# An attention kernel on one core: the weighted sum and the work-bank task change places in three of four slots

## The reference

```
q = heads(x @ Wq);  k_s, v_s = heads(x @ Wkv_short);  k_l, v_l = heads(x @ Wkv_long)
decay_bias = -|i - j| * (1 - decay_factor)
out = alpha * softmax(q k_s^T / 4 + decay_bias) v_s + (1 - alpha) * softmax(q k_l^T / 4) v_l
x = layernorm(x + out @ Wo)
c = sigmoid(xt wf + c uf + bf) * c + sigmoid(xt wi + c ui + bi) * tanh(xt wc + c uc + bc)   # over the 16 sequences
x = layernorm(x + tanh(x wo + c_final uo + bo))
```

## Time and profile before

| | |
|---|---|
| median of 3 runs | 2131.12 us (2130.34 to 2136.34) |
| the profiled execution, its own time | 2128.4 us |
| its span | 2126.6 us |
| PE busy | 2004.9 us (94%) |
| DVE busy | 1532.1 us (72%) |
| ACT busy | 1458.0 us (69%) |
| POOL busy | 254.4 us (12%) |
| exponential, 128x1024, without and with bias unit scale | 1024 and 1114 ns |
| maximum, 128x1024 | 1221 ns |
| `keep_sums` copy, `vals` copy, `kq_h` copy | 598, 383, 593 ns |
| `kq_l` | 691 ns |

### The profile page before, as it was taken

One profiled execution on the slowest core, in us unless ns is written; L12 is line 12 of the kernel. 1 busy time (PEld: TensorE's weight loads), 2 busy tenths in 40 slices (PEclk: granted clock), 3 DMA queues, 4 the chain that ended last, 5 costly groups with the idle time before them and its releaser, 6 DMA issues.

```text
span 2126.6 us, 40587 instructions
## 1 busy us (share of the span) xinstructions
PE 2004.9 (94%) x15776; PEld 1055.1 (50%) x15776; DVE 1532.1 (72%) x1826; ACT 1458.0 (69%) x1750; POOL 254.4 (12%) x284
## 2 busy tenths in 40 slices
PE   6999999999999999999999999999999878999997
PEld 3444444444444444444444444444444336888887
DVE  6777878878787878787878787878787743333346
ACT  2777777777777777777777777777777662333337
POOL 0001111111111111111111111111111011000014
PEclk7999999999999999999999999999999999999999
DMA  4233333333333333333333333333323411000017
GB/s 112 63 78 77 87 77 87 78 87 78 86 79 85 80 85 79 85 80 85 81 84 80 84 82 83 82 85 81 84 70 86 114 53 40 30 30 31 30 61 257
DMA packets 157060, 170.00 MB, mean 80 GB/s; under 512 B 72756, under 2 KB 92980, under 8 KB 156868
## 3 DMA queue, kind: packets, MB, share of 16 engines
q1 hardware_dynamic: 132740, 133.61, 25.2%
q10 hardware_dynamic: 24128, 33.79, 5.1%
HBM read 54.55 MB, written 17.83 MB: 34 GB/s over the span
## 4 chain that ended last, share of the span: by engine, by line
PE 74%; ACT 8%; issue 6%; DVE 6%; SPq 4%; DMA 1%; ACTq 1%; POOL 0%; DVEq 0%; POOLq 0%
PE pv_ps L772 15%; PE work L676 14%; PE pair_ps L708 14%; PE banks L1163 12%; PE pair_ps L734 12%; ACT probs L443 7%; DVE maxes L633 3%; PE pair_ps L684 3%; PE banks L1203 2%; SPq L241 2%; DVE stats L619 1%; DVE res L615 1%; SPq L246 1%; SPq L303 1%; PE banks L1210 1%
## 5 line engine op out<-in xcount | busy, mean ns | idle before, releaser
L633 DVE TENSOR_REDUCE maxes<-pair_ps 128x2 fp32r<-128x1024 f32 x1024 | 1228.0, 1221 | 294.4 <-PE pair_ps L684 164.6
L443 ACT ACTIVATE probs<-pair_ps,small 128x1024 f32<-128x1024 f32 x512 | 563.4, 1114 | 221.3 <-PE pair_ps L684 218.7
L443 ACT ACTIVATE probs<-pair_ps 128x1024 f32<-128x1024 f32 x512 | 513.2, 1024 | 113.9 <-PE pair_ps L708 105.4
L772 PE MATMUL pv_ps<-probs,vals 128*32 128x512 f32 x4096 | 548.7, 608 | 11.1 <-ACT pv_sb L477 10.8
L708 PE MATMUL pair_ps<-q_op,k_op 56*128 56x512 f32 (+1 forms) x2048 | 479.8, 477 | 31.1 <-DVE maxes L633 16.2
L734 PE MATMUL pair_ps<-k_op,q_op 55*128 55x512 f32 x2048 | 451.7, 440 | 40.6 <-ACT probs L443 26.0
L708 PEld LDWEIGHTS pair_ps<-q_op,k_op 56*128 56x128 f32 (+1 forms) x2048 | 193.0, 185 | 461.8 <-DVE maxes L633 219.7
L734 PEld LDWEIGHTS pair_ps<-k_op,q_op 55*128 55x128 f32 x2048 | 196.8, 187 | 213.5 <-issue 105.1
L684 PE MATMUL pair_ps<-eye_b,tri_b 64*128 64x64 bf16 x4096 | 164.3, 194 | 0.0
L684 PEld LDWEIGHTS pair_ps<-eye_b,tri_b 64*128 64x128 bf16 x4096 | 94.9, 96 | 116.2 <-issue 97.7
L772 PEld LDWEIGHTS pv_ps<-probs,vals 128*32 128x32 f32 x4096 | 81.3, 108 | 112.5 <-issue 98.5
(11 more groups left out here) (148 smaller groups left out, 2080.4 us busy)
## 6 DMA issues: line engine op xcount, KB each, us to landing
k_op<-kq_h SPq DMA_DIRECT2D x508, 64.0 KB, 2.2
q_op<-kq_h SPq DMA_DIRECT2D x256, 64.0 KB, 2.3
o_att<-pv_sb SPq DMA_DIRECT2D x512, 32.0 KB
inverses<-inv_dram SPq DMA_DIRECT2D x64, 256.0 KB
k_op<-kq_l SPq DMA_DIRECT2D x254, 64.0 KB, 2.3
x_step<-in_xT ACTq DMA_DIRECT2D x16, 512.0 KB, 4.2
q_op<-kq_l SPq DMA_DIRECT2D x128, 64.0 KB, 2.3
q_op<-shift_rows SPq DMA_DIRECT2D x512, 2.0 KB
```

The lines of the kernel that those rows point to most:

```text
L443: act.activation(probs[:, s % 2, 2 * hp:2 * hp + 2, :], pairs_ps[pair_of(b, s, "b", hp)][:, :, :], ACT.Exp, scale=LAM if s // 4 % 2 else 1 ...
L633: dve.reduce_max(maxima[u % 2][:, :, hp, s % 4], pairs_ps[pair_of(b, s, "a", hp)][:, :, :], mybir.AxisListType.X).then_inc(a_reduced, 1)
L772: last = pe.matmul(pv_ps[32 * h:32 * h + 32, :], vals[:, c, g // 2, att, at:at + 32], probs[:, s % 2, h, :], start=(c == 0), stop=(c == TC ...
```

## The change

In the slots with c = 0, 2 and 3, PE issues `weigh_before` where `work_task` stood (behind the scores of pair 0) and `work_task` where `weigh_before` stood (behind the scores of pair 1). The part of the slot with c = 1 stays. On ACT the task's part goes behind the exponential of pair 1. On DVE it goes behind the maximum of pair 1 in every slot (it stood there already with c = 0).

```diff
@@ ACT, body
                     if exists(b):
                         exp_pair(b, s, 0)
-                    part_or_values(b, s)
                     if exists(b):
                         exp_pair(b, s, 1)
+                    part_or_values(b, s)
@@ DVE, body
                     reduce(0)
                     if s % TC == 0:
                         turn(*unit_of(b, s // 4 + 1))
-                        reduce(1)
+                    reduce(1)
                     if has_task(b, s):
...
-                    if s % TC:
-                        reduce(1)
@@ PE, body
                     bias_for_max(b, s, 0)
-                    work_task(b, s)
+                    weigh_before(b, s)
                     scores(b, s, 1)
                     scores_for_max(b, s, 1)
                     bias(b, s, 1)
                     bias_for_max(b, s, 1)
-                    weigh_before(b, s)
+                    work_task(b, s)
...
                     bias_for_max(b, s + 2, 0)
-                    work_task(b, s + 2)
+                    weigh_before(b, s + 2)
                     scores(b, s + 2, 1)
...
-                    weigh_before(b, s + 2)
+                    work_task(b, s + 2)
                     scores(b, s + 3, 0)
...
-                    work_task(b, s + 3)
+                    weigh_before(b, s + 3)
                     scores(b, s + 3, 1)
...
-                    weigh_before(b, s + 3)
+                    work_task(b, s + 3)
```

## The result

The changed kernel takes 2152.8 us (median of 4 runs, 2152.11 to 2153.02), against 2130.7 us for the one before (2128.41 to 2136.34): by the means 1.0099 times as long, 95% interval 1.0079 to 1.0119. The forecast was 2152.6 us, +21.5 where +22.1 came. The profiled execution took 2153.0 us, its span 2151.2.

What follows compares the result with a forecast made beforehand. The prediction took PE as the bound. Its terms sum to 1.4 us per sequence, 21 us over fifteen, plus 0.5 in the last: 2131.1 + 21.5 = 2152.6 us; own range 2145 to 2167.

Steps and rivals of the forecast that it cites:

- PE is the bound, and small standstills add up: PE, whole sequence: it stands still about 6 us per sequence in small pieces, and small delays are not made good later.
- The new V adds no wait for its exponential: PE, V issued 1.6 us earlier: the fill ahead already needed the same exponential, so added wait 0.
- the fills lose and gain 0.1 us by V and W and come out at 0: PE fills: those with W in place of V lose 0.1 us, others gain it; in odd units 0 net.
- The copy ahead of `keep_sums` in slots 24 and 28: ACT: the moved copy delays keep_sums and chunk 1's exponentials, +0.35 us in slot 24 and +0.3 in slot 28.
- the relief of b2.1: PE, units 8, 24 and 28: b2.1's lateness behind a late exponential goes with V1 ahead of it, -0.1 us each.
- The same in slots 0 and 4: ACT: the moved copy delays keep_sums, +0.3 us in slot 0 and +0.2 in slot 4.
- My step for slot 4: ACT: keep_sums goes from 805.65 to 806.05, but the next exponential had 0.18 us of waiting: +0.2 us.
- The `kq_h` copy ahead of b0.0's exponential: ACT, between b3.1's exponential and b0.0's: up to 0.25 us of lateness, mostly covered; 0.1 us per sequence put on it.
- DVE in unit 16: DVE: later kq_l delays the maxima of a0.1 and a1.0, so b2.0 comes later by +0.25 us.
- Slots 7 and 8: PE, slots without W: waits move to a0.0, b1.0 and b1.1; taken as 0, and -0.1 us for b2.1.
- The clock: Rival: PE's clock falls in part of the stretch; one sequence of it is +100 us, 2253 us. Chance 0.01.
- The faster rival: Waits in slots 7 and 8 go, 1.7 us per sequence: -25 us, 2106, or 2127 if the added terms hold. Chance 0.13.

Runs made afterwards that it cites:

- the thin copies: Changed kernel with only one head in eight of the value copies in slots with c = 0: 2146.3 us, ratio 1.0065 to the kernel before.
- their control: The kernel before with only one head in eight of the value copies in slots with c = 0: 2130.1 us, ratio 0.9996.
- the collisions on ACT mended: Changed kernel, x converted in slot 6, last normalise in slot 30, keep_sums ahead of copy: 2129.2 us; kernel before, last normalise in slot 30: 2122.4 us.
- the fastest kernel with the order of before: Kernel before with normalise in slots 24, 26, 27 and 30 and high_part in slots 10 and 31: 2118.4 us, ratio 0.9938.

## Why the prediction was right, step by step

- **PE is the bound, and small standstills add up.** Held in the main. Same instructions, same durations, +1.58 us per sequence of standing still; 1.4 was forecast. That nothing is made good later is too strong: of the 0.36 us lost in the column of slot 4, 0.31 come back in the next.
- **The new V adds no wait for its exponential.** Held: the lists of waits of the changed kernel name no such wait at `pv_ps`, only `keep_sums`. The step beside it, that the fills lose and gain 0.1 us by V and W and come out at 0, left out a0.0 of an even unit behind an odd one: there 0.1 is lost (below).
- **The copy ahead of `keep_sums` in slots 24 and 28.** Held, as the thin copies and their control show. The forecast was 0.35 + 0.3 with the relief of b2.1 counted; the columns ahead of these V0 rose by 0.49 + 0.33.
- **The same in slots 0 and 4.** Mis-sized: 0.3 and 0.2 were forecast. In slot 0 V0 waits 0.13 us, and thin copies gave 0.12 back there; in slot 4 V0 doesn't wait, and they gave nothing back. I charged 0.4 us from the copy's start to that of the next instruction. The rows show 0.28 (910.71 to 910.99 in slot 0, 812.50 to 812.78 for slot 3's copy) and 0.26 (896.36 to 896.62 in slot 28): on ACT an instruction that is ready starts 0.11 to 0.12 us before the end of the one ahead. The Trainium skill, "ScalarE: Activation LUTs", section "What ACT_TABLE_LOAD costs", gives an overlap of about 93 ns for back-to-back activations. These rows agree within 0.03 us. I had read durations where starts were to be had.
- **Slot 4, the step that I missed.** Slot 3's copy and the conversion of x come ahead of b0.0's exponential: 0.44 us, by the run that moved the conversion. My step for slot 4 said 0.2 by another way. I followed the copies of slots with c = 0 and not that of slot 3 into the slot behind it.
- **The `kq_h` copy ahead of b0.0's exponential.** 0.1 was set on it. The rows show it in slot 28 alone, where `normalise` of slot 27 stands behind the copy: b0.0's exponential starts 1.10 us behind b0.0's load (893.57, 892.47) where it was 0.86 (881.87, 881.01), and a0.1 comes 0.44 us behind b0.1 in place of 0.32. No run isolates it.
- **DVE in unit 16.** Wrong in its cause and in its size: +0.25 was forecast for `kq_l` in DVE's queue, with b2.0 later by as much. The period that ends with V0 of slot 16 grew by 0.15 and b2.0's wait by 0.06 (1.26 to 1.32), but shortening `kq_l` brought nothing back. By the rows 0.11 of it is a0.0's wait for the exponential of b3.1, behind a W in place of a V. No run isolates this wait.
- **Slots 7 and 8.** Held, with the three waits in the named places, and +0.05 for the two periods together. (The 1.62 us between the four fills without bias, less 0.90 for three, are 0.7 us of lateness; the prediction has 0.6 in one place and 0.7 in another, and its sum uses neither.) The faster rival failed at the point that was named for it, a0.0 of slot 8.
- **The clock.** The granted clock is 1.00 from 392 to 1660 us in both kernels and in the twelve others, with more standstills than before; that rival is out.

So the near match of the total is in part luck. Slot 0 (0.3 against 0.14) and unit 16 (0.25 against 0.15) were too high, slot 4 (0.2 against 0.38, from a step that was not in the sum) and slots 24 and 28 (0.65 against 0.82) too low, and the errors largely cancel. The upper end of the forecast's own range, 2167 us, has no sum behind it in the prediction.

The measured account of the +1.58 is this. With the collisions on ACT mended in both orders as far as each has them, the sequences take 105.66 (after) and 105.31 (before, `normalise` in slot 30): 0.35 is left for the rest of the new order, and the other 1.23 are the copies, the conversion and what they push. The two mended kernels don't differ by exactly the change, and by the launches (ratios 0.9992 and 0.9956) the rest is 0.5 and not 0.35, so that the split is good to 0.2 or so. (Against the fastest kernel with the order of before, at 105.01, it would be 0.65, but that one moves instructions on ACT which have no match in the other.) The columns of the 0.35 are +0.38 (slot 4), -0.33 (slot 8), +0.13 (slot 12), +0.12 (slot 24) and 0.07 or less for each other one. The rows name a cause for three places, the run of fills in slots 7 and 8, a0.0 of unit 16 and a0.1 of slot 28; no run tests them, and this part stays open.

## What to carry to other kernels

When work is swapped in an order written by hand, follow what its consumers queue in front of: halving the length of five short copies was worth nothing where they ran in the idle time of ACT, and 0.67 us per sequence where they stood one instruction later. Take the time from start to start, and try the thinned operation in both orders, since that tells cover from cost directly. Half of a change can cost three times the whole if the whole preserves a distance (here between two users of one bank) that the half breaks.

## What the runs showed of the hardware that was not expected

An instruction on ACT that is followed by a ready one occupies it for 0.11 to 0.12 us less than its row says. A copy of 0.38 or 0.39 us takes 0.26 or 0.28 from start to start, and behind `keep_sums`, whose row says 0.60, the exponential starts after 0.49 (897.73 to 898.22 in slot 28). For a short copy this is a third of its row.

A wait that is listed can be worth much less than it says when the queue behind it is full. Without V0's waits of 1.4 us per sequence only 0.46 came back: the column of slot 24 fell by 0.89, and that of slot 28 rose by 0.84. With the copies one slot later, the wait appeared three fills on, 1.36 us ahead of b2.1 with 0.84 of streaming in it.
